# A two-pass group norm, binary 3x3 convolution and scale map on one core: six statistics blocks on ScalarE instead of three, and a last group finished bank by bank

## What is computed

```python
def _gn(v, G=32, eps=1e-5):              # group norm over 8 channels and 56x56
    g = v.reshape(B_, G, C_ // G, H_, W_)
    m = jnp.mean(g, axis=(2, 3, 4), keepdims=True); s = jnp.var(g, axis=(2, 3, 4), keepdims=True)
    return ((g - m) / jnp.sqrt(s + eps)).reshape(v.shape)

def _L0_conv_ref(x, gamma, beta, w, b, bb):     # applied to _gn(x)
    mean = jnp.mean(x, axis=(0, 2, 3), keepdims=True)
    var = jnp.mean(jnp.square(x - mean), axis=(0, 2, 3), keepdims=True)
    xn = (x - mean) * lax.rsqrt(var + 1e-4) * gamma + beta
    t = where(xn <= 0, -1, where(xn >= 0, 1, 0))             # signs
    xc = jnp.clip(xn, -1, 1)
    y = conv3x3(t, w) + b
    beta_map = (conv3x3_ones(sum_c(xc * t)) + bb) / (conv3x3_ones(sum_c(abs(t))) + bb)
    return y * beta_map

out = x + _L0_conv_ref(_gn(x), ...)
```

## Time and profile before

| | us |
|---|---|
| median of 3 runs | 935.04 (934.71 to 936.57) |
| the profiled execution | 934.54 |
| its span, first to last instruction | 932.7 |
| outside the span | 1.8 |
| busy: PE, DVE, ACT, POOL | 782.7, 779.0, 600.6, 141.4 |
| mean DMA rate over the span | 250 GB/s |

### The profile page before, as it was taken

One profiled execution on the slowest core, in us unless ns is written; L12 is line 12 of the kernel. 1 busy time (PEld: TensorE's weight loads), 2 busy tenths in 40 slices (PEclk: granted clock), 3 DMA queues, 4 the chain that ended last, 5 costly groups with the idle time before them and its releaser, 6 DMA issues. The chain is left out here.

```text
span 932.7 us, 12739 instructions
## 1 busy us (share of the span) xinstructions
PE 782.7 (84%) x4686; PEld 464.9 (50%) x4686; DVE 779.0 (84%) x1217; ACT 600.6 (64%) x490; POOL 141.4 (15%) x160
## 2 busy tenths in 40 slices
PE   2100005999999999999999999999999999999996
PEld 2100003555555555555555555555555555555553
DVE  4999888899888888888888979797879787979755
ACT  2042636868777777777777777777768686868310
POOL 0089400011111111111011111111111111101011
PEclk9655556999999999999999999999999999999998
DMA  9999972369888888888887869696969696958489
GB/s 358 430 405 379 419 325 81 135 180 286 256 243 229 250 227 248 229 237 248 220 266 202 288 174 315 166 316 159 312 168 303 172 291 188 290 157 215 131 214 269
DMA packets 43478, 232.79 MB, mean 250 GB/s; under 512 B 10560, under 2 KB 10688, under 8 KB 39360
## 3 DMA queue, kind: packets, MB, share of 16 engines
q0 software_dynamic: 18144, 101.16, 42.1%
q1 hardware_dynamic: 24544, 131.25, 38.7%
q10 hardware_dynamic: 768, 0.12, 0.1%
HBM read 180.73 MB, written 51.79 MB: 249 GB/s over the span
## 5 line engine op out<-in xcount | busy, mean ns | idle before, releaser
L606 PE MATMUL acc<-V,U 128*128 128x385 f16 (+1 forms) x4608 | 769.4, 330 | 11.8 <-DVE V L832 10.1
L606 PEld LDWEIGHTS acc<-V,U 128*128 128x128 f16 x4608 | 451.0, 98 | 325.6 <-issue 12.8
L477 ACT ACTIVATE sn<-acc,inv_s 128x784 f32<-128x784 f32 x128 | 116.9, 913 | 206.8 <-PE acc L606 200.9
L350 POOL DMA_DIRECT2D y<-x x63 | 53.9, 856 | 724.6 <-DVE y L919 711.4
L919 DVE SCALAR_TENSOR_TENSOR y<-y,vec,bmap 128x1568 f32<-128x1568 f32 (+1 forms) x65 | 117.6, 1810 | 0.2
L455 ACT ACTIVATE r<-xb,ab 128x1568 f32<-128x1568 f32 x64 | 106.6, 1690 | 6.3 <-ACT u L430 4.0
L430 ACT ACTIVATE u<-xb,ab 128x1624 f16<-128x1624 f32 x63 | 109.0, 1732 | 0.2
L440 ACT ACTIVATE T<-u 128x1680 f16<-128x1680 f16 x60 | 95.6, 1594 | 2.2 <-DVE D L826 2.2
L443 ACT ACTIVATE T<-T 128x1568 f16<-128x1568 f16 x58 | 87.6, 1511 | 1.8
L579 PE MATMUL csum<-mv,cst 128*128 128x32 f32 x2 | 0.6, 397 | 90.7 <-DVE mv L690 90.7
L826 DVE TENSOR_TENSOR D<-T 128x1568 f16<-128x1568 f16 x63 | 61.3, 973 | 15.3 <-ACT T L443 15.0
(11 more groups left out here) (110 smaller groups left out, 414.8 us busy)
## 6 DMA issues: line engine op xcount, KB each, us to landing
xb<-x SPq DMA_DIRECT2D x64, 812.0 KB, 6.5
y<-x POOLq DMA_DIRECT2D x63, 784.0 KB, 8.0
out<-y POOLq DMA_DIRECT2D x63, 784.0 KB, 9.3
y<-x SPq DMA_DIRECT2D x16, 1568.0 KB, 8.7
bmap<-map_rows SPq DMA_DIRECT2D x32, 784.0 KB, 6.4
xb<-x SPq DMA_DIRECT2D x14, 1568.0 KB, 10.2
V<-w_t SPq DMA_DIRECT2D x2, 1152.0 KB, 14.7
out<-y SPq DMA_DIRECT2D x2, 392.0 KB, 3.0
```

The costliest lines, as they stand in the source:

```text
L477: nc.scalar.activation(sn[:, b, half], acc[:, b, :, 0:N], ACT.Copy, scale=inv_s[:, b:b + 1])\
L606: last = nc.tensor.matmul(by_row(acc[:, g % 2, bank, 0:N])[:, :, lo:hi], U[:, ci, digits, k, dx, co * P:(co + 1) * P], by_row(V[:, a, ci, ...
```

## The change

1. `ACT_BLOCKS` becomes (4, 8, 16, 21, 25, 29): six blocks on ACT, 26 on DVE. ACT does blocks 4 and 8 ahead of its weight steps (before block 8 it hasn't begun them), block 16 between the two input halves of the weights, and 21, 25, 29 after them.
2. The last piece of the last load (g = 3 of image 0) comes as two transfers, its first 15 rows with a semaphore of their own (`x_upper`) and its other 14 rows. DVE reads two of its four parts after the first, two after the second.
3. Group 2 of the last image gets x from `xb` on DVE (`add_x(2)`) and is stored by SP; POOL's accumulating transfer and store for it go.
4. Group 3 of the last image: PE's order becomes first(bank 0), third(2), first(bank 1), second, third. Each snapshot of it is two of 392 elements, with a semaphore for bank 0, so that SECOND and THIRD may start with bank 0 while bank 1 is copied. DVE makes `ds` bank by bank, adds row 0 of every four when THIRD has ended in bank 0, finishes and stores rows 0 to 2 of every four (`LAST_ROWS`), then does row 3 alone.

```diff
-ACT_BLOCKS = (21, 24, 27)
-LAST_PARTS = ((0, N // 2), (N // 2, N))
+ACT_BLOCKS = (4, 8, 16, 21, 25, 29)
+LAST_ROWS = ((0, 3), (3, 4))
@@ sync: image 0
-                    load_rows(x_rows[0], g)
+                    if g == 3:
+                        first = (HR - 1) * W
+                        sp.dma_start(xb[:, 1, 1, 0:UPPER * W], x_rows[0, 1][:, first:first + UPPER * W])\
+                          .then_inc(x_upper, 16)
+                        sp.dma_start(xb[:, 1, 1, UPPER * W:XR * W], x_rows[0, 1][:, first + UPPER * W:first + XR * W])\
+                          .then_inc(x_in[3], 16)
+                    else:
+                        load_rows(x_rows[0], g)
@@ sync: the last stores
+            sp.wait_ge(last_added, 1)
+            sp.dma_start(out_v[NI - 1, 0, 1], y[:, 2]).then_inc(last_out[2], 16)
+            for k, (lo, hi) in enumerate(LAST_ROWS):
+                sp.wait_ge(last_added, k + 2)
+                sp.dma_start(quads(out_v[NI - 1, 1, 1])[:, :, lo:hi].rearrange("p q i w -> p q (i w)"),
+                             quads(y[:, 3])[:, :, lo:hi].rearrange("p q i w -> p q (i w)")).then_inc(last_out[k], 16)
@@ gpsimd
-            for s in range(G4 * NI - 1):
+            for s in range(G4 * NI - 2):
...
-            store(G4 * NI - 2)
+            store(G4 * NI - 3)
@@ scalar
+            statistics(0)
+            statistics(1)
             for ci in range(CT):
...
+                if ci == 0:
+                    statistics(2)
+            for j in range(3, len(ACT_BLOCKS)):
+                statistics(j)
...
+            snapshot(last, 2, 1)
+            act.wait_ge(mid_done, G4 * NI - 2)
+            for half, done, part_done, snap, part_snap in ((0, first_done, first_half, snap1, snap1_half),
+                                                           (1, second_done, second_half, snap2, snap2_half)):
+                for bank in range(2):
+                    if bank:
+                        act.wait_ge(done, G4 * NI)
+                    else:
+                        act.wait_ge(part_done, 1)
+                    nc.scalar.activation(sn[:, 1, half, bank], acc[:, 1, bank, 0:N], ACT.Copy, scale=inv_s[:, 1:2])\
+                      .then_inc(snap if bank else part_snap, 1)
@@ tensor: products, between the banks
+                        if half is not None and bank == 0:
+                            last.then_inc(half, 1)
+                            if planes is SECOND:
+                                pe.wait_ge(snap1, G4 * NI)
+                            if planes is THIRD:
+                                pe.wait_ge(snap2, G4 * NI)
@@ tensor: image
+                    last = final and g == 3
+                    if last:
+                        first(n, a, g, banks=(0,), half=first_half)
+                    else:
+                        first(n, a, g)
                     if g == 0:
                         quarter_sums(n)
                     third(n - 1, 1 - a, 3) if g == 0 else third(n, a, g - 1)
-                    second(n, a, g)
+                    if last:
+                        first(n, a, g, banks=(1,))
+                    second(n, a, g, second_half if last else None)
@@ vector: the statistics skip ACT_BLOCKS below 12 too; the end
+            def last_mid():
+                last = G4 * NI
+                for bank in range(2):
+                    if bank:
+                        dve.wait_ge(snap2, last)
+                    else:
+                        dve.wait_ge(snap2_half, 1)
+                        dve.wait_ge(y03_done, last - 1)
+                    ins = nc.vector.scalar_tensor_tensor(out=ds[:, bank], in0=sn[:, 1, 0, bank], scalar=2.0,
+                                                         in1=sn[:, 1, 1, bank], op0=ALU.mult, op1=ALU.subtract)
...
+            def last_end(k):
+                if k:
+                    dve.wait_ge(third_done, G4 * NI)
+                else:
+                    dve.wait_ge(third_half, 1)
...
-            mid(NI - 1, 3)
-            ends(NI - 1, 3)
+            add_x(2)
+            last_mid()
             for k in range(2):
-                finish(NI - 1, 3, LAST_PARTS[k])
-                add_last(k)
+                last_end(k)
+                last_finish(k)
```

More of the change, by code:

```diff
@@ L369, in _, with statistics @@
                                      wt[:, c].rearrange("p a b o -> p (a b o)"), ACT.Abs).then_inc(w_abs, 1)
+            def statistics(j):
+                k = ACT_BLOCKS[j]
+                m, a, c = stat_image(k)
+                act.wait_ge(s_in[a][c], 16 * (k // 4) + 16)
+                nc.scalar.activation(stat_buffer(a, c), stat_buffer(a, c), ACT.Copy, accum_out=sums[:, j, 0:1])\
+                  .then_inc(act_sum, 1)
+                act.wait_ge(act_sum, j + 1)
+                nc.scalar.activation(mv[:, m, c, 0:1], sums[:, j, 0:1], ACT.Copy, scale=1.0 / (H * W))
+                nc.scalar.activation(sums[:, j, 1:2], sums[:, j, 0:1], ACT.Copy, scale=-1.0 / (H * W))\
+                  .then_inc(act_mean, 1)
+                act.wait_ge(act_mean, j + 1)
+                nc.scalar.activation(stat_buffer(a, c), stat_buffer(a, c), ACT.Square, bias=sums[:, j, 1:2],
+                                     accum_out=sums[:, j, 2:3]).then_inc(act_read, 1)
+                act.wait_ge(act_read, j + 1)
+                nc.scalar.activation(mv[:, m, c, 1:2], sums[:, j, 2:3], ACT.Copy, scale=1.0 / (H * W))\
+                  .then_inc(act_var, 1)
+            statistics(0)
+            statistics(1)
             for ci in range(CT):
@@ L552, in _ @@
             channel_sums(last)
-            for g in range(1, G4):
+            for g in range(1, G4 - 1):
                 snapshot(last, g - 1, 1)
                 snapshot(last, g, 0)
-            snapshot(NI - 1, 3, 1)
+            snapshot(last, 2, 1)
[9 more added lines that the diff above has]
+                      .then_inc(snap if bank else part_snap, 1)
         @block.tensor
@@ L592, in quarter_sums, with products @@
                                  cst[:, C_FOLD:C_FOLD + SQ], start=True, stop=True).then_inc(cs_done, 1)
-            def products(n, a, g, planes, done, by_channels=False, banks=(0, 1)):
+            def products(n, a, g, planes, done, by_channels=False, banks=(0, 1), half=None):
                 h, co = g // 2, g % 2
@@ L611, in products, with first, second @@
                                 stop=(planes is THIRD and i == len(TERMS) - 1), skip_group_check=True)
+                        if half is not None and bank == 0:
[4 more added lines that the diff above has]
+                                pe.wait_ge(snap2, G4 * NI)
                 if 1 in banks:
                     last.then_inc(done, 1)
-            def first(n, a, g, by_channels=False, banks=(0, 1)):
+            def first(n, a, g, by_channels=False, banks=(0, 1), half=None):
                 if 0 in banks:
                     at_least(pe, y03_done, 4 * n + g - 1)
[L619 to L624, removed]
+                products(n, a, g, FIRST, first_done, by_channels, banks, half)
+            def second(n, a, g, half=None):
+                if half is None:
+                    pe.wait_ge(snap1, 4 * n + g + 1)
+                else:
+                    pe.wait_ge(snap1_half, 1)
+                products(n, a, g, SECOND, second_done, half=half)
             def third(n, a, g):
@@ L629, in third, with image @@
                 products(n, a, g, THIRD, third_done)
-            def image(n, a):
+            def image(n, a, final=False):
                 for g in range(G4):
@@ L662, in _ @@
                 image(2 * i + 2, 0)
-            image(NI - 1, 1)
-            third(NI - 1, 1, 3)
+            image(NI - 1, 1, final=True)
+            pe.wait_ge(snap2_half, 1)
+            products(NI - 1, 1, 3, THIRD, third_done, half=third_half)
         @block.vector
@@ L710, in last_statistics @@
                 for h in range(2):
-                    dve.wait_ge(x_in[2 * h + c], 16)
+                    dve.wait_ge(x_upper if h and c else x_in[2 * h + c], 16)
                     for j in range(4):
+                        if h and c and j == 2:
+                            dve.wait_ge(x_in[3], 16)
                         ins = nc.vector.bn_stats(st[:, 0, c, 4 * h + j], own_rows(2 * h + c)[:, j * N:(j + 1) * N])
@@ L718, in _ @@
             for k in range(8):
-                statistics(k)
+                if k not in ACT_BLOCKS:
+                    statistics(k)
             dve.wait_ge(wall, 1)
@@ L910, in ends, with finish @@
                 ins.then_inc(y03_done, 1)
-            def finish(n, g, part=None):
+            def finish(n, g):
                 s, b, h = 4 * n + g, g % 2, g // 2
-                lo, hi = (4 * at for at in part or (0, N))
                 dve.wait_ge(mid_done, s + 1)
@@ L918, in finish @@
                 dve.wait_ge(bmap_in[h], 16 * n + 16)
[L919 to L924, removed]
```

(17 more changed lines are left out.)

45 lines of the change are left out of this document (20 added, 25 removed).

## The result

The changed kernel takes 926.35 us (median of 5 runs, 924.86 to 928.24) against 934.74 us before (5 runs, 933.69 to 936.57): ratio 0.9908, 95% interval 0.9895 to 0.9920, so 8.4 us or 0.9% faster. The profiled execution took 926.35 us with a span of 924.6, where before it was 934.54 and 932.7.

| | before | after | |
|---|---|---|---|
| last aggregate of the statistics ends | 140.40 | 134.61 | -5.8 |
| from there to the first product | 12.13 | 12.13 | 0 |
| first product to the snapshot after the last SECOND | 766.80 | 766.98 | +0.2 |
| from there to the end of DVE's last addition | 10.41 | 7.70 | -2.7 |
| from there to the end of the span | 2.96 | 3.18 | +0.2 |

The account below looks back on a forecast made before the run. PE bounds the main pass; in the statistics pass transfers are the floor, DVE just above. Savings of 2.1 + 1.8 + 2.6 = 6.5 us take the profiled 934.54 to 928.0, median forecast 928.5, range 925.6 to 931.8.

Parts of the forecast that it names:

- the rival that all of the rate comes back: Loads from 60 to 84 us regain all 3.6 us; 8.3 us saved in all, median 926.7; chance 0.15.
- The sign named for the head: End of the statistics pass: DVE's last aggregate ends at 136 to 137 us, against 140.40 before.
- The middle as one block: Small-step chain and main pass: 12.1 us to the first product unchanged; everything behind it moves one for one.
- DVE's lateness at image 0: End of the statistics pass: DVE starts image 0's first piece 2.1 us late; with block 29 on ACT, 2.1 saved.
- The rate: Loads from 60 to 84 us, at 366 GB/s: earlier transfers save 1.8 us, the middle of 0 and 3.6.
- ACT holds no load up: Statistics pass: ACT frees buffers 8.7 us ahead, which is enough; block 21's next load up to 4 us late at worst.
- The split costs and gains nothing: Last piece of image 0: DVE arrives after all of it has landed, so two transfers change nothing; zero.
- The end: After the last SECOND: DVE's chain ends 2.8 us sooner, the last store queues 0.2 us more; 2.6 us saved.
- Small pieces: Last two stores: 0.017 and 0.033 us a packet; rival of 0.112 us each makes the median 938.2, chance 0.04.
- The memory limit: Statistics pass: the skill's 358 GB/s would leave part 1 no gain, 932.4; contradicted by 432 GB/s, no chance given.

Follow-up runs that it names:

- late_three: The kernel before with ACT blocks 21, 25 and 29 instead of 21, 24 and 27, no split, old end; 932.75 us, one run.
- early_two_more: The kernel before with blocks 4 and 8 on ACT as well as 21, 24 and 27, no split, old end; 930.01 us, one run.
- block_22: The changed kernel with block 22 on ACT instead of 21 and the last piece of image 0 in one transfer; 926.87 us, one run.
- column_end: The changed kernel with bank by bank snapshots kept, but rows 0 and 3 added before two halves by columns, stored in 3136-byte pieces; 927.51 us, one run.
- late_four: The kernel before with blocks 16, 21, 25 and 29 on ACT, no split, old end; 931.55 us, one run.
- end_only: The kernel before with only the new end: old ACT blocks 21, 24, 27 and no split; 931.69 us, ratio 0.9957.

## Why the prediction was right or wrong

Right in sign, and 926.35 lies in the range of 925.6 to 931.8, 2.2 us under the 928.5 forecast; what came was the rival that all of the rate comes back (926.7), to which the prediction gave 0.15. The sign named for the head, a last aggregate at 136 to 137, was missed (134.61), by the size of one term.

- **The middle as one block**: held. 12.13 us from the last aggregate to the first product in both; the main pass moved by 0.2 us. Over all kernels here it took 766.3 to 768.3 us, 2 us of scatter by itself, which is why small effects are read from distances in the traces and not from single times.
- **DVE's lateness at image 0, 2.1 us**: held, 2.2 in `late_three`; before the change the piece landed at 129.81 and DVE started it at 131.96. DVE needed 8.48 us from there (8.44).
- **The rate, 1.8 us**: this is the step that failed, in its size. It measured 3.6 us in the changed kernel (5.8 less 2.2; 3.9 in `early_two_more`, and 3.7 by the landing of image 0's first piece), which is the upper bound of 24 x (1 - 366/430) = 3.6; kernels with equal statistics differ by up to 0.6 us. I had taken the middle of 0 and 3.6, since only the idle share, 1.2 us, looked curable, and engines that are busy look as if an earlier issue could give them nothing. The kernels with early loads show that the slow packets went away along with the idle time. I had also said that the trace couldn't tell why they were slow. It could have told more: how long before the last landing each load was issued, and that 86 in a hundred of the packets ran at full speed.
- **ACT holds no load up**: held. 8.7 us ahead was enough: the loads behind blocks 4, 8, 16 and 25 land 8.6 to 9.0 us after they are issued and 3.7 after the load before them (no load waits for block 29). Block 21 was late as foreseen, and cost 0 to 0.3 us (`block_22`), not the up to 4 us that I had set aside.
- **The split costs and gains nothing**: held.
- **The end, 2.6 us**: held; 2.71 on DVE less 0.22 at the last store. DVE's chain ended 7.70 after the snapshot, forecast 7.7. Undone alone, the bank by bank snapshots cost 0.88 and the rows 1.02 on DVE; that is 1.9 of the 2.71, and how the other 0.8 falls between them when both are undone wasn't tried. Both experiments leave a third part of the new end in place: row 0 is added as soon as THIRD has ended in bank 0, where the old kernel waited for both banks. In `column_end` row 3 starts at 918.13, when both banks are ready; had row 0 waited as well, row 3 would have come 0.54 us later by the rows of before (925.04 - 924.50), an estimate that would cover most of the rest.
- **Small pieces**: 0.017 and 0.033 us for the two sizes made 2.8 us for both stores, and 2.8 is what the engines took (0.017 and 0.039 us a packet). The last store, in rows of 224 bytes, ends 0.2 us later after DVE's last addition than the old 3136-byte pieces did. The Trainium skill, DMA: Bandwidth & Descriptors, section Specifications, has the engine read, modify and write below 512 bytes. The one us more that I had estimated from this doesn't come; whether such a cost is inside the 0.017 us no run here can tell.
- **The memory limit.** Every kernel here held 427 to 434 GB/s from 36 to 48 us. The Trainium skill, in the same section, gives about 358 GB/s for a core, worked out as half of a stack's 716. The traces don't agree with it as a limit for one core that runs by itself, as here.

## What to carry to other kernels

Where transfers are the floor of a stretch, look at when each load is issued, not only at whether the reader keeps up: a reader that is 4 us late with giving buffers back cost 3.6 us of landing, though DVE was never idle and the engines were busy at 95%. Giving the second engine one early block (8) cured it, giving it one late (16) didn't, and moving its last two blocks from 24 and 27 to 25 and 29 was worth 2.2 us with no work saved. At the very end, split what the last engine waits for by the unit in which the engine before it finishes, here a PSUM bank, and let the output follow that split even if its pieces are small.

## What was not expected of the hardware

Late loads made packets slow and not only absent. From 60 to 84 us the engines were busy at 0.95 in `late_four` and moved 368 GB/s, which is 387 per full share; with early loads it was 432 at 1.01. The slowness sits in a minority of packets, 12 to 16 in a hundred, which took over 0.5 and up to 2.4 us instead of 0.47. Why packets are slow when a queue is refilled late isn't settled by these runs, nor how early is early enough. It was so in all four kernels with load 16 issued at 69.6 to 69.9 (before, `end_only`, `late_three`, `late_four`), and in none of the nine with it at 65.4 to 66.3.

A mean rate isn't a landing time. In the changed kernel load 22 landed 4.73 us after load 21, one us more than the usual spacing, while the stretch from 84 to 100 us ran at 428 GB/s; load 25 landed on the usual spacing while 100 to 124 us ran at 412.
